# Scores of the second attention layer on row tiles, a pair of heads at a time

## The reference

```python
Q = (input_Q @ W_Q.T + b_Q).reshape(batch, -1, NUM_HEADS, D_K).transpose(0, 2, 1, 3)
K = (input_K @ W_K.T + b_K).reshape(batch, -1, NUM_HEADS, D_K).transpose(0, 2, 1, 3)
V = (input_V @ W_V.T + b_V).reshape(batch, -1, NUM_HEADS, D_V).transpose(0, 2, 1, 3)
scores = jnp.einsum('bhqd,bhkd->bhqk', Q, K) / np.sqrt(D_K).astype(np.float32)
scores = jnp.where(attn_mask[:, None, :, :], jnp.float32(-10000.0), scores)
attn = jax.nn.softmax(scores, axis=-1)
out = jnp.einsum('bhqk,bhkd->bhqd', attn, V)
...
x = x + jnp.tanh(g_xattn[1]) * _L1_xattn_ref(_layernorm(x, axis=-1), ctx_1024, ctx_1024, mask_BxSxS2_bk1, ...)
```

## Time and profile before

| | |
|---|---|
| median of 3 runs | 267.69 us (267.55 to 268.81) |
| profiled execution, its time | 269.31 us |
| its span | 267.3 us |
| PE busy (matmuls) | 252.2 us, 94% |
| PE weight loads | 198.7 us, 74% |
| DVE, ACT, POOL busy | 79%, 71%, 68% |
| granted clock of PE, mean | 0.998 |

### The profile page before, as it was taken

The page is one execution under the profiler, slowest core; times in us unless marked ns, Lnnn a source line. Parts: engine busy times, 40 slices in busy tenths (PEclk is TensorE's granted clock), DMA queues, the critical chain, the costliest instruction groups (busy, mean ns, idle before and its releaser), DMA issues. The chain is left out here.

```text
span 267.3 us, 6698 instructions
## 1 busy us (share of the span) xinstructions
PE 252.2 (94%) x1899; PEld 198.7 (74%) x1899; DVE 210.1 (79%) x654; ACT 188.5 (71%) x451; POOL 181.7 (68%) x272
## 2 busy tenths in 40 slices
PE   7997999999788999999999999999999999999894
PEld 4664667777557777778777888777787778999893
DVE  3899899999999896799667877777798625995573
ACT  2488889998799777857776867677788564544562
POOL 5667999985889665745844575449758795954380
PEclk9999999999999999999999999999999999999999
DMA  6458352300025854645584766756552051212530
GB/s 204 154 156 284 143 194 85 120 0 4 1 46 117 183 111 101 142 94 121 124 214 119 185 174 177 195 134 174 131 139 52 17 147 39 78 43 81 165 98 20
DMA packets 25475, 31.86 MB, mean 119 GB/s; under 512 B 4000, under 2 KB 18144, under 8 KB 25312
## 3 DMA queue, kind: packets, MB, share of 16 engines
q1 hardware_dynamic: 25008, 31.23, 43.3%
q10 hardware_dynamic: 432, 0.22, 0.3%
HBM read 14.32 MB, written 2.42 MB: 63 GB/s over the span
## 5 line engine op out<-in xcount | busy, mean ns | idle before, releaser
L637 POOL TENSOR_SCALAR probs<-probs,rsum 128x512 f32<-128x512 f32 x128 | 88.3, 696 | 49.9 <-DVE rsum L996 49.1
L783 ACT ACTIVATE probs<-masked,neg_max 128x512 f32<-128x512 f32 x128 | 91.7, 718 | 11.8 <-DVE neg_max L987 8.8
L1320 PE MATMUL bank<-ident,probs 128*128 128x128 f32 x512 | 78.5, 276 | 2.6 <-DVE probsT L1004 1.2
L1320 PEld LDWEIGHTS bank<-ident,probs 128*128 128x128 f32 x512 | 58.7, 141 | 19.2 <-issue 10.3
L987 DVE CUSTOM_DVE_ANT_0 masked<-bank,mask 128x512 f32<-128x512 f32 x64 | 43.8, 684 | 15.2 <-PE bank L1456 14.6
L792 ACT ACTIVATE probsT<-bank 128x512 f32<-128x512 f32 x74 | 43.6, 589 | 15.1 <-PE bank L1320 14.7
L1493 PE MATMUL bank<-probsT,val 128*32 128x256 f32 (+1 forms) x512 | 46.6, 384 | 0.0
L1004 DVE COPY probsT<-bank 128x512 f32<-128x512 f32 x54 | 36.7, 680 | 8.8 <-PE bank L1320 8.6
L987 DVE CUSTOM_DVE_ANT_0 masked<-bank,shared 128x512 f32<-128x512 f32 x64 | 43.3, 677 | 0.1
L1493 PEld LDWEIGHTS bank<-probsT,val 128*32 128x32 f32 (+1 forms) x512 | 24.4, 123 | 18.0 <-issue 4.8
L1449 PE MATMUL bank<-parts 128*128 128x512 f32 x64 | 31.1, 486 | 1.6 <-DVE neg_max L987 1.3
(11 more groups left out here) (254 smaller groups left out, 517.8 us busy)
## 6 DMA issues: line engine op xcount, KB each, us to landing
k_both<-k_low SPq DMA_DIRECT2D x32, 128.0 KB, 3.0
k_both<-k_high SPq DMA_DIRECT2D x32, 128.0 KB, 2.8
q<-q_split SPq DMA_DIRECT2D x32, 128.0 KB, 2.4
probsT<-staged_gate SPq DMA_DIRECT2D x32, 128.0 KB, 3.0
q<-q_split SPq DMA_DIRECT2D x32, 64.0 KB, 2.1
parts<-staged_k SPq DMA_DIRECT2D x7, 256.0 KB, 2.7
w_flat<-in_w SPq DMA_DIRECT2D x1, 1536.0 KB, 7.2
staged_q<-q_split SPq DMA_DIRECT2D x4, 256.0 KB, 2.6
```

What stands on the lines that cost most here:

```text
L637: pool.tensor_scalar(p, p, rsum[:, u % NCOL:u % NCOL + 1], 1.0, ALU.mult, ALU.mult).then_inc(normed, 1)
L783: act.activation(probs[:, u % NP, :], masked[:, u % NS, :], ACT.Exp, scale=-1.0, bias=neg_max[:, c:c + 1], accum_out=sums[:, c:c + 1]).the ...
L1320: ins = pe.transpose(dst[0:rows, t * P:t * P + P], src, ident[:, :])
```

## The change

The scores of the second layer are issued for a pair of units, both heads of one query tile, in every other iteration (`score_pair`): three matmuls for each head, all on that head's own 64 rows, the two heads alternating, into the two score banks. The pair waits for the maxima of both banks. For that the units of a block change their order (query tile slowest), and DVE takes the two masked maxima of a pair one after the other in every other iteration. The stacked copies, their DMAs, their semaphores, the zeros in `q1_high` and the waits for them are gone; ACT, DVE and PE wait for earlier scores and for the jobs themselves instead. `k1_low` and `q1_split` get three slots, and the memory that was shared with later parts is now its own (`later`, `hid_parts`). The q job of block 8 moves from iteration 52 to 54, that of block 9 from 56 to 57. Of the hunks left out, one drops `turns_of_stack`, one two lists of semaphores, and two replace 10 by 8 in a wait for `late_ready`.

```diff
@@ -126,7 +126,7 @@
     for k in BLOCKS[8:]:
         early = 1 if k.m == 10 else 0
         plan.setdefault(k.first - early - (14 if k.m == 9 else 13 if k.g or k.b else 15), []).append(("k", k.m))
-        plan.setdefault(k.first - early - (12 if k.m < 10 else 11), []).append(("q", k.m))
+        plan.setdefault(k.first - early - (10 if k.m == 8 else 11), []).append(("q", k.m))
     for n, name in enumerate(("kn", "qn", "v0")):
         plan.setdefault(LN01_AT + 7 + 2 * n, []).append((name, 1))
     for two in range(8):
...
@@ -233,7 +228,10 @@
 def unit(u):
 
     k = [k for k in BLOCKS if k.first <= u < k.end][0]
-    return (k, *divmod(u - k.first, NQ))
+    if k.layer == 0:
+        return (k, *divmod(u - k.first, NQ))
+    qt, h = divmod(u - k.first, k.heads)
+    return k, h, qt
 
 
 def build(nc, a, out):
@@ -317,12 +315,11 @@
         bo1 = sb("bo1", [P, P])
         mask1 = sb("mask1", [P, B, NQ, SK], BF16)
         k1_high = sb("k1_high", [P, NKQ, SK], F32R)
-        k1_low = sb("k1_low", [P, 2, SK], F32R)
-        q1_split = sb("q1_split", [P, 2, 2, SQ], F32R)
-        k1_both = sb("k1_both", [P, NKQ, 2, SK], F32R)
+        k1_low = sb("k1_low", [P, NKQ, SK], F32R)
+        q1_split = sb("q1_split", [P, NKQ, 2, SQ], F32R)
+        later = sb("later", [P, 2048], F32R)
         high_k, high_q = k1_high[:, 2, :], x1_high[:, 0:SQ]
-        q1 = sb("q1", [P, NKQ, 2, 2, SQ], F32R)
-        q1_high, q1_both = q1[:, :, :, 0, :], q1[:, :, :, 1, :]
+        hid_parts = sb("hid_parts", [P, 2, RING, 2 * SQ], F32R)
 
         small = sb("small", [P, 5 * P])
         fw, fq, fwT = (small[:, P * i:P * i + P] for i in range(3))
@@ -366,14 +363,11 @@
-        q1_flat = q1[:, :, :, :, :].rearrange("p s h n q -> p (s h n q)")
-        hid_high, hid_low = (q1_flat[:, 6 * SQ * i:6 * SQ * (i + 1)].rearrange("p (i t) -> p i t", i=RING) for i in range(2))
+        hid_high, hid_low = hid_parts[:, 0, :, :], hid_parts[:, 1, :, :]
-        low_flat = k1_low[:, :, :].rearrange("p i k -> p (i k)")
-        query_flat = q1_split[:, :, :, :].rearrange("p i n q -> p (i n q)")
         ctx_flat = ctx_parts[:, :, :].rearrange("p n c -> p (n c)")
-        homes = [t[:, c:c + 512] for t, begin, end in ((parts, 3072, 6144), (early, 0, 3072), (low_flat, 0, 1024), (query_flat, 0, 1024),
+        homes = [t[:, c:c + 512] for t, begin, end in ((parts, 3072, 6144), (early, 0, 3072), (later, 0, 2048),
                                                        (parts, 0, 3072), (ctx_flat, 0, 2048)) for c in range(begin, end, 512)]
...
@@ -547,28 +539,9 @@
 
             own = [slice(64 * h, 64 * h + 64) for h in range(2)]
 
-            def stack_k(k):
-                i, s = k.m % 2, k.m % NKQ
-                sp.wait_ge(*freed(("k", k.m)))
-                sp.wait_ge(scored, BLOCKS[k.m - NKQ].end)
-                for h in range(2):
-                    sp.dma_start(k1_both[own[h], s, h, :].bitcast(F32), k1_low[own[h], i, :].bitcast(F32)).then_inc(k_stacked[s], 16)
-                    sp.dma_start(k1_both[own[1 - h], s, h, :].bitcast(F32), k1_high[own[h], s, :].bitcast(F32)).then_inc(k_stacked[s], 16)
-
-            def stack_q(k):
-                i, s = k.m % 2, k.m % NKQ
-                sp.wait_ge(*freed(("q", k.m)))
-                sp.wait_ge(scored, BLOCKS[k.m - NKQ].end)
-                for h in range(2):
-                    sp.dma_start(q1[own[h], s, h, :, :].bitcast(F32),
-                                 q1_split[own[h], i, 0, :].bitcast(F32).unsqueeze(1).to_broadcast([64, 2, SQ])).then_inc(q_stacked[s], 16)
-                    sp.dma_start(q1_both[own[1 - h], s, h, :].bitcast(F32),
-                                 q1_split[own[h], i, 1, :].bitcast(F32)).then_inc(q_stacked[s], 16)
-
             for t in sorted(PLAN):
                 for j in PLAN[t]:
                     if j[0] in ("k", "q") and BLOCKS[j[1]].layer == 1:
-                        (stack_k if j[0] == "k" else stack_q)(BLOCKS[j[1]])
                         n = j[1] - PIECES_FROM
                         if j[0] == "q" and 0 <= n < 9:
                             w, name, part = (we1, we3, we2)[n % 3], ("we1", "we3", "we2")[n % 3], EXPERT_PIECES[n // 3]
@@ -663,10 +636,7 @@
                     pool.wait_ge(scored, TOTAL // 2)
                 elif n < 12:
                     pool.wait_ge(job_done, jobs_done(range(4)))
-                elif n < 16:
-                    for m in (22, 23):
-                        pool.wait_ge((k_stacked if n < 14 else q_stacked)[m % NKQ], 64 * turns_of_stack(m))
-                else:
+                elif n >= 16:
                     pool.wait_ge(job_done, jobs_done(range(8)))
                 w = (we1, we3, we2)[which][:, 2 * d:min(2 * d + 2, HALVES), :].rearrange("p e c -> p (e c)")
                 split(expert_step(0, which, d), expert_step(1, which, d), w, weights_split)
@@ -720,8 +690,6 @@
                         power_of(2, b)
                 if 0 <= t + LEAD - 3 < TOTAL:
                     norm(t + LEAD - 3)
-                if t in (8, 10):
-                    publish_late(pool.memset(q1_high[:, :, t // 10, :].bitcast(F32), 0.0))
                 if t in (10, 43):
                     scale_bias(int(t > 10))
                 for b in range(B):
@@ -813,7 +781,7 @@
                 if name in ("k", "q"):
                     k = BLOCKS[j[1]]
                     cols = SK if name == "k" else SQ
-                    i, row = k.m % 2, slice(k.g, k.g + 1)
+                    i, row = k.m % NKQ, slice(k.g, k.g + 1)
                     if k.layer == 0:
 
                         high, sign, bias = ((high_q, lo_q, minus_bq0), (high_k, lo_k, minus_bk0))[name == "k"]
@@ -822,15 +790,10 @@
                                        scale=sign[:, 0:1]).then_inc(high_ready, 1)
                         return
                     bias = (bq1, bk1)[name == "k"]
-                    if name == "k":
-                        act.wait_ge(scored, BLOCKS[k.m - NKQ].end)
-                        high = k1_high[:, k.m % NKQ, :]
-                    else:
-                        if k.m < 10:
-                            act.wait_ge(q_staged[k.m - 8], 32)
-                        else:
-                            act.wait_ge(q_stacked[(k.m - 2) % NKQ], 64 * turns_of_stack(k.m - 2))
-                        high = q1_split[:, i, 0, :]
+                    act.wait_ge(scored, BLOCKS[k.m - NKQ].end)
+                    if k.m in (9, 10):
+                        act.wait_ge((k_staged if name == "k" else q_staged)[k.m - 9], 32)
+                    high = k1_high[:, i, :] if name == "k" else q1_split[:, i, 0, :]
                     act.activation(high, job_bank[:, 0:cols], ACT.Identity, bias=bias[:, row]).then_inc(high_ready, 1)
                 elif name == "kn":
                     act.activation(k1_high[:, j[1], :], job_bank[:, :], ACT.Identity, bias=bk0[:, 0:1]).then_inc(high_ready, 1)
@@ -1045,17 +1008,12 @@
                             return
                         return
                     dve.wait_ge(high_ready, HIGHS[j])
+                    dve.wait_ge(scored, BLOCKS[k.m - NKQ].end)
+                    if k.m in (9, 10):
+                        dve.wait_ge((k_staged if name == "k" else q_staged)[k.m - 9], 32)
                     if name == "k":
-                        if k.m < 10:
-                            dve.wait_ge(k_staged[k.m - 8], 32)
-                        else:
-                            dve.wait_ge(k_stacked[(k.m - 2) % NKQ], 64 * turns_of_stack(k.m - 2))
-                        low, bank_in, bias, high = k1_low[:, i, :], job_bank[:, :], bk1, k1_high[:, k.m % NKQ, :]
+                        low, bank_in, bias, high = k1_low[:, i, :], job_bank[:, :], bk1, k1_high[:, i, :]
                     else:
-                        if k.m < 10:
-                            dve.wait_ge(q_staged[k.m - 8], 32)
-                        else:
-                            dve.wait_ge(q_stacked[(k.m - 2) % NKQ], 64 * turns_of_stack(k.m - 2))
                         low, bank_in, bias, high = q1_split[:, i, 1, :], job_bank[:, 0:SQ], bq1, q1_split[:, i, 0, :]
                     dve.scalar_tensor_tensor(out=low, in0=bank_in, scalar=bias[:, row], in1=high.bitcast(F32),
                                              op0=ALU.add, op1=ALU.subtract).then_inc(free, 1)
...
@@ -1247,8 +1205,11 @@
             for t in range(-LEAD, EXPERTS_AT):
                 if t + LEAD - 1 == TOTAL // 2:
                     dve.wait_ge(mask_ready[1], B * NQ)
-                if 2 <= t + LEAD - 1 < TOTAL:
+                if 2 <= t + LEAD - 1 < L1_AT:
                     mask_max(t + LEAD - 1)
+                if L1_AT <= t + LEAD - 1 < TOTAL and t % 2:
+                    mask_max(t + LEAD - 1)
+                    mask_max(t + LEAD)
                 if 0 <= t + LEAD - 3 < TOTAL:
                     recip(t + LEAD - 3)
                 for j in PLAN.get(t - 1, ()):
@@ -1447,13 +1408,21 @@
                     else:
```

(26 more changed lines are left out.)

8 lines of the change are left out of this document (2 added, 6 removed).

## The result

The changed kernel takes 278.60 us (median of 4 runs, 276.69 to 278.79) against 267.64 (4 runs, 267.55 to 268.81): the medians stand 11.0 us apart, the ratio is 1.037 with a 95% interval from 1.034 to 1.040. It is slower, as forecast, but outside the range of 260.0 to 276.7. The profiled execution has 278.49 us, with a span of 276.6. Experiments 1 to 8 ran on one chip, 9 and 10 on a second, 11 and 12 on a third, and which chip the changed kernel's runs had is not on record; so against the changed kernel or another chip each is first compared with the median of the kernel before beside it (268.26 for experiments 1 to 4, 268.19 for 5 to 8, 268.71 for 9 and 10, 268.51 for 11 and 12).

The account below looks back on a forecast made before the run. The prediction took PE's issue time to bound the second layer's scores, and DVE the first layer. It added +5.0 us for the scores and +1.0 for the seam to the median 267.7, giving 273.7 us, range 260 to 276.7.

Parts of the forecast that it names:

- Direction and main mechanism: Whole kernel: slower, chance 0.62; main case, chance 0.53, row tiles cost more in visits than they save, 273.7 us.
- 0.40 a visit: Second layer's scores on PE: going from whole array to row tiles and back costs 0.40 us, bounds 0 and 0.40.
- run together in 0.23: Scores of a pair: two row tiles share one 512-column step of 0.23 us, upper bound 0.46; 0.69 a pair.
- +5.0 us: Second layer's scores: 0.69 + 0.40 - 0.93 a pair, +0.16 for 28 pairs and +0.12 for four.
- rival 1: Second layer's scores: row tiles cost no entry and loads run ahead, giving 261 to 262.5 us; chance 0.28.
- Stacking: Stacked copies: dropping 128 DMAs brings nothing in the stage, only the one wait of 0.38 us at the first scores.
- Both banks: PE's wait for both maxima before a pair: costed at nothing, up to 0.1 us a pair (3 us) as upper bound.
- rival 3: Second layer's stage: waiting for both banks holds PE up, 8 us on top of the main case, 281.7; chance 0.06.
- The seam: Passage to the second layer's scores at unit 64, where DVE is the bound: +1.0 us, bounds 0 and 2.
- some 0.4: First pair at the seam: waiting for unit 63's maximum costs some 0.4 us, about the DMA wait that goes.
- The meeting of the jobs: Seam: q job of block 8 shares iteration and bank with block 9's k job; DVE waits some 1.5 us, +1.0.
- the slack of 0.2 us: Pair followed by a value job: DVE finishes both maxima with 0.2 us to spare before PE wants the banks.

Follow-up runs that it names:

- experiment 1: Changed kernel with the q jobs of blocks 8 and 9 back in iterations 52 and 56: 276.94 us, ratio 1.032.
- experiment 2: Changed kernel with each pair's scores as four 128-row matmuls instead of six of 64, high-low products left out: 270.90 us, ratio 1.011.
- experiment 3: Changed kernel with all three matmuls of one head issued before those of the other: 278.52 us in one run.
- experiment 4: Kernel before with pairs, a wait for both banks and maxima in pairs; no row tiles, stacked copies kept: 272.37 us, ratio 1.016.
- experiment 5: experiment 1 plus score banks of units 62 and 63 exchanged, so the first pair needs only unit 62's maximum: 274.26 us, ratio 1.023.
- experiment 6: experiment 4 plus the exchange of score banks of units 62 and 63: 269.32 us, ratio 1.005.
- experiment 7: experiment 5 with layer two's mixes, but the last, one iteration earlier, right behind a pair: 272.60 us, ratio 1.016.
- experiment 8: Changed kernel with only the score banks of units 62 and 63 exchanged, q jobs where the change put them: 276.00 us, ratio 1.029.
- experiment 9: Changed kernel with eight dummy matmuls into the free bank before the first pair's wait for unit 63: 277.92 us, ratio 1.038.
- experiment 10: experiment 5 with the turn right behind the pair, ahead of the jobs and the projection: 274.35 us, ratio 1.022.
- experiment 11: Changed kernel with four dummy matmuls into the free bank before the first pair's wait for unit 63: 276.61 us, ratio 1.031.
- experiment 12: experiment 7 with the turn right behind the pair in a block's other pair iteration: 273.02 us, ratio 1.017.

## Why the prediction missed

**Direction and main mechanism: right.** The forecast's 0.40 a visit was put together from column tiles; the rows after give 0.39 (0.18 to 0.19 for the way in with the first load, 0.09 out, 0.11 for the load behind). Two tiles of a step were taken to run together in 0.23: it is 0.24 in the rows. For "+5.0 us" there are 5.0 between the stages of experiments 6 and 5, 4.9 between their medians, and 5.4 from the rows of experiment 2. The rule of the Trainium skill that a change of tiling mode drains the engine (TensorEngine Tiling (Array Packing), Key Properties) is borne out here for row tiles as for column tiles, and experiment 7 bears it out between the two; the page has no price, and the 0.39 is this kernel's. What decided against rival 1 is the row of weight loads: the first load stands at 152.51 with its matmul, not ahead of it.

**Stacking: right inside the stage.** 128 DMAs and 14.7 MB less (31.86 to 17.18 MB) brought nothing there: 123.8 us with and without them. No experiment takes the copies alone away, so what they are worth at the seam isn't shown.

**Both banks, inside the stage: right.** There is no wait of PE on neg_max from 100 to 215 us, so rival 3 is out; the 1.1 us of experiment 6 are what pairs cost once the first of them is free, where nothing was forecast and 3 us allowed. Where they arise stays open.

**The seam: the step that failed.** "The first pair needs the maximum of unit 63, which DVE does in that same iteration, and holds PE and then DVE up by some 0.4, about the DMA wait that goes. Together +1.0 us, bounds 0 and 2." The meeting of the jobs, forecast as +1.0 by a DVE wait of 1.5, costs 1.7 (experiments 5 and 8) with a DVE wait of 1.78: mis-sized by 0.7. The "0.4" is wrong by far more: the wait is 1.83 us. It could have been read from the trace of before. DVE's timeline there, from the maximum of unit 63 on (the next one takes the mask of layer two, so it is unit 64's):

```profile
87.12 0.68 DVE L987 CUSTOM_DVE_ANT_0 masked<-bank,shared 128x512 f32<-128x512 f32 x1
87.73 0.09 DVE L987 DVE_READ_ACCUMULATOR2_ANT neg_max<- 128x1 f32 x1
...
87.80 0.67 DVE L987 CUSTOM_DVE_ANT_0 masked<-bank,mask 128x512 f32<-128x512 f32 x1
```

PE began the first scores at 86.46, after a wait of 0.38, so it was free at 86.08; the maximum of unit 63 was read at 87.82. A PE that must wait for it stands for 1.7 us. In layer one DVE is the bound and runs behind PE by that much, and the slack of 0.2 us that I had worked out for a pair holds in the stage, where PE is the bound and DVE waits for it. I had taken the slack of one stage into another.

**The clock: put at nothing, without a reason.** The sum has no term for it; the 1.00 was read from windows in which PE was busy throughout or nearly. A wait of 1.8 us stood ahead of a fall of the granted clock from 1.00 to 0.50 in the profiled executions of the changed kernel and of experiments 1 and 4, though not in that of experiment 2; in those of experiments 3 and 9 the fall came behind the other stop of the seam, of 1.4 us. Within one kernel an execution with the fall took about 2 us more than the one without (278.49 to 278.79 against 276.69), and filling the wait gives 2.0 back (experiment 11).

The 11.0 us, then, each step over the kernel before beside it: pairs in free banks 1.1 (experiment 6), visits and all else of the tiles 4.9 (to experiment 5), jobs that meet 1.7 (to 8), and the bank of unit 63 with its clock 3.1 (to the changed kernel), of which the clock is about 2. The last step reaches to the changed kernel, whose chip isn't known, and is the least certain; on one chip, experiments 1 and 5, it is 2.7. The steps don't add up everywhere: by them experiment 2, which has all but the tiles, would stand 6.1 above the kernel before, or some 4 without the clock, and it stands 2.6 above. This remainder of about 1.5 us stays open. Had the seam cost the 1.0 that I gave it, the time would have stood within the range; it cost 4.8. Even the upper bounds together (2 for the seam, 3 for both banks) give only 277.7.

## What to carry to other kernels

Going to row tiles and back cost 0.39 us a visit here, and it is paid by the visit, not by the matmul: count visits, ask what is saved in each (0.24 us here, so it lost), and put two visits to tiles of different kinds next to each other (1.7 us won in 15 places). Where an edit adds a wait, size it at the seams between stages too, from the starts that the trace of before shows for both sides, since another engine may be the bound there. And where an edit makes PE stop, price the clock behind the stop as well: here it cost about as much again as the 1.8 us stop itself, and dummy matmuls into a free bank were cheaper. Look at the granted clock of every execution before taking a median: one kernel can have executions with the fall and without.
